# GpSimd instead of VectorE makes the sixteen sums of the base weights' quadrants

## Chip, cores and metric

One core of one Trainium2 chip runs the program. The metric is the device time of one execution in microseconds (us), as the median of the runs shown. Engines are named as in the profile: PE (TensorE matmul), PEld (its weight load), DVE (VectorE), ACT (ScalarE), POOL (GpSimd), SP (the queue that issues most DMAs).

## What is computed

```python
q_emb = relu(cond @ W3 + b3)                      # 16 x 1024
v_sum = sum(x, axis=1)                            # x: 16 x 512 x 1024
y = relu(((512 * x + v_sum) * q_emb[:, None]) @ W2 + b2)
base = y @ W_base + b_base
shared = (y @ A_s) @ B_s
gates = softmax(y @ W_router + b_router)          # 6 experts, the best two kept
routed = sum over e of ((y @ A_r[e]) * w_e) @ B_r[e]
out = x + base + shared + routed
```

Both 1024 x 1024 products, with W2 and with W_base, take nearly all the work. The other terms are of rank 16 to 112.

## The kernel before, in words

The 16 batches go in 8 pairs through a W2 stage (pair numbers g = 0 to 7, i = g in the code) and then again 8 pairs through a W_base stage (g = 8 to 15, p = g - 8). Activations lie transposed, features on partitions, 512 tokens in a row. A pair and a weight matrix, each cut in two by two quadrants, are multiplied in the Strassen-Winograd way: 7 products n = 0 to 6 in place of 8, each of 4 tiles in, 4 tiles out (`group(g, n, j)`, output tile j). Some pairs replace some of these products by another such step inside (`inner`). Every operand of a product is split in a high part rounded to fp32r (made by ACT, `high`, `wb_high`) and the rest (made by DVE, `low`, `wb_low`), and each tile product is three matmuls: high x high, low x high, high x low (`three`, lines 3062 to 3064). So a group is 12 matmuls.

The weights of W_base for the seven products are the quadrants themselves (n = 0, 1, 6) and four sums of quadrants, each made in four tiles k of 128x512. They are made while the last pair of the W2 stage (i = LAST = 7) and the first of the W_base stage (g = 8, p = 0) run:

- `wb_sum_1(k)`: Q21 + Q22, in place in `wl_raw[:, 2]`, the weights of product 3.
- `wb_sum_2(k)`: that less Q11, again in place, for product 2. It waits until `wb_low(3, k)` has read the first sum, and for Q11, which SP loads into `wh_raw[:, 2]` once all four `wb_sum_1` are counted (`sp.wait_ge(wb_sum, H)`, line 653).
- `wb_sum_4(k)`: Q12 less the tile of `wb_sum_2`, for product 4.
- `wb_sum_3(k)`: Q11 - Q21, for product 5.

One semaphore, `wb_sum`, counts all sixteen in this order, and `wb_high` on ACT waits for it (lines 1242 to 1259). `wl_raw` and `w_lo` have the same addresses, and so have `wh_raw` and `w_hi`: `wb_low(2, k)` overwrites the tile that `wb_sum_4(k)` reads. `wb_high(2, k)` stands in ACT's program between the `high(8, 0, j)` of the next pair and `y_high(7, C22, j)`, so what it waits for holds these up too.

The order of the work on each engine is written out by hand; engines meet at semaphores alone. On DVE, between the second and the last output tiles of pair 7, stand in turn `low(8, 0, j)`, `y_low(7, C22, j)`, `c21(7, j - 1)`, `t1(8, j)` and a sum. `y_low` (line 2048 for C22 and C21, line 2046 for C11 and C12) makes the low part of an output tile of the W2 stage, and PE's `project_y` (three matmuls, the router's and the experts' first factor) takes it directly behind one group: PE does group(7, 6, 0), project_y(7, C22, 0), group(7, 6, 1), project_y(7, C22, 1) and so on to project_y(7, C22, 3), and then group(8, 0, j), project_y(7, C21, j). The `c22` and `c21` steps (line 1991) add a PSUM bank to a tile in SBUF.

GpSimd makes a few small column vectors (`shift_of`, `shift2_of`) and issues DMAs of the inner steps' weights. In its program, between its last `shifts(7)` and the first `store_weights(7)`, stands nothing.

Of the kernel before, what the change touches and what calls it, by code (L numbers as in the profile page):

```python
# [7 lines left out]
ALU = mybir.AluOpType  # L8
# [19 lines left out]
H = 4  # L28
# [9 lines left out]
def adaln_ffn(nc, xT, condT, w3, w2, b2, wbase, bbase, acat, bcat, brouter, outT, E, R):  # L38
# [9 lines left out]
    LAST = NP - 1  # L48
# [10 lines left out]
    with ExitStack() as ctx:  # L59
# [47 lines left out]
        wh_raw = sb("wh_raw", [P, NPROD, H, T], F32, early)  # L107
        wl_raw = sb("wl_raw", [P, NPROD, H, T], F32, early)
# [768 lines left out]
        def _(pool):  # L877
# [128 lines left out]
            for e in range(EARLY):  # L1006
# [5 lines left out]
                if e + 1 < EARLY:  # L1012
                    load_partner(e + 1)
                    shift_of_partner(e + 1)
                    shifts(i + 2)

            for c in range(L2, 2 * L2):
                store_weights(c)
            for e in range(EARLY, len(QUADS)):
# [843 lines left out]
        def _(dve):  # L1863
# [339 lines left out]

            def wb_low(n, k):
                dve.wait_ge(wb_hi_done, wb_no(n, k))
                nc.vector.tensor_tensor(w_lo[:, n, k, :], wl_raw[:, 2 if n == 3 else n, k, :],
                                        w_hi[:, n, k, :].bitcast(F32), ALU.subtract).then_inc(wb_lo_done, 1)

# [12 lines left out]
            def inner_weight_sums(late):  # L2221
# [10 lines left out]
                nc.vector.tensor_tensor(iq11, iq22, iq11, ALU.subtract).then_inc(inner_w_sum, 1)  # L2232
                dve.wait_ge(inner_w_sum, sums_no(late, 3))
                nc.vector.tensor_tensor(iq12, iq12, iq11, ALU.subtract).then_inc(inner_w_sum, 1)

            def wb_sum_1(k):
                dve.wait_ge(wl_loaded[2], 16)
                dve.wait_ge(wh_loaded[2], 16)
                nc.vector.tensor_tensor(wl_raw[:, 2, k, :], wl_raw[:, 2, k, :], wh_raw[:, 2, k, :],
                                        ALU.add).then_inc(wb_sum, 1)  # L2240

            def wb_sum_2(k):

                dve.wait_ge(wb_lo_done, wb_lo_no(3, k))
                dve.wait_ge(wh_loaded[2], 32)
                nc.vector.tensor_tensor(wl_raw[:, 2, k, :], wl_raw[:, 2, k, :], wh_raw[:, 2, k, :],
                                        ALU.subtract).then_inc(wb_sum, 1)

            def wb_sum_4(k):
                dve.wait_ge(wb_sum, H + k + 1)  # L2250
                dve.wait_ge(wl_loaded[4], 16)
                nc.vector.tensor_tensor(wl_raw[:, 4, k, :], wl_raw[:, 4, k, :], wl_raw[:, 2, k, :],
                                        ALU.subtract).then_inc(wb_sum, 1)

            def wb_sum_3(k):
                dve.wait_ge(wl_loaded[5], 16)
                dve.wait_ge(wh_loaded[5], 16)
                nc.vector.tensor_tensor(wl_raw[:, 5, k, :], wl_raw[:, 5, k, :], wh_raw[:, 5, k, :],
                                        ALU.subtract).then_inc(wb_sum, 1)

            def inner_t1(r):
                e, n = RUNS[r]
# [292 lines left out]
            def pair(i):  # L2555
                if i == 0:
                    first_pair()
                else:
                    before_p4(i)
                    for j in range(H):  # L2560
                        low(i, 4, j)
                        if j == 1 and i not in QUADS:
                            gate_weights(i - 1, GA)
                        elif j == 2:
                            gate_apply(i - 1, GB)
                    if i in QUADS:
                        gate_logits(i - 1, GA)
                    y_low(i, C11, 0)
                    y_low(i, C11, 1)
                    if i == 1:  # L2570
                        inner_weight_low(0)
                        inner_weight_low(1)
                    if i == LAST:
                        for k in range(H):
                            wb_low(0, k)
                    for j in range(H):
                        low(i, 5, j)
                        if i in QUADS and j == 0:
                            gate_weights(i - 1, GA)
                        if j in (1, 2):  # L2580
                            y_low(i, C11, j + 1)
                        if i == LAST:
                            wb_sum_1(j)
                        if i == 1 and j == 0:
                            inner_weight_low(2)
                        elif i == 1 and j == 1:
                            inner_weight_sums(0)
                        elif i == 1 and j == 3:
                            inner_weight_low(3)
                    y_low(i, C12, 0)  # L2590
                    y_low(i, C12, 1)
                    for j in range(H):
                        low(i, 6, j)
                        if j == 0 and i == 1:
                            gate_apply(i - 1, GA)
                        if j > 0:
                            c22(i, j - 1)
                        if j >= 2:
                            y_low(i, C12, j)
                        if i == LAST:  # L2600
                            wb_low(3, j)
                        if i == 1 and j != 1:
                            inner_weight_low((4, 4, 5, 6)[j])
                    if i == LAST:
                        wb_low(1, 0)
                        wb_low(1, 1)
                    c22(i, H - 1)
                y_low(i, C22, 0)
                if joined(i):
                    gate_apply(i - 1, GA)  # L2610
                if i == LAST:
                    wb_sum_2(0)
                if i == 0:
                    c21(0, 0)
                    y_low(0, C22, 1)
                    low(1, 0, 0)
                    t1(1, 0)
                    low(1, 0, 1)
                    y_low(0, C22, 2)
                    c21(0, 1)  # L2620
                    low(1, 0, 2)
                    y_low(0, C22, 3)
                    low(1, 0, 3)
                    c21(0, 2)
                    for j in range(1, H):
                        t1(1, j)
                else:
                    for j in range(H):
                        low(i + 1, 0, j)
                        if j > 0 and i == LAST:  # L2630
                            y_low(i, C22, j)
                            c21(i, j - 1)
                        elif j > 0:
                            c21(i, j - 1)
                            y_low(i, C22, j)
                        t1(i + 1, j)
                        if i == LAST and j < H - 1:
                            wb_sum_2(j + 1)
                    if i == LAST:
                        wb_low(1, 2)  # L2640
                        wb_low(1, 3)
# [201 lines left out]
            def alone(p):  # L2843
                g = NP + p
                if p == 0:
                    y_low(LAST, C21, 0)
                for j in range(H):
                    low(g, 1, j)
                    if p == 0 and j > 0:
                        y_low(LAST, C21, j)  # L2850
                    t2(g, j)
                    if p == 0:
                        wb_sum_4(j)
                for j in range(H):
                    low(g, 2, j)
                    if p == 0 and j == 0:
                        gate_logits(LAST, GB)
                    if j == H - 1:
                        if p == 0:
                            dve.wait_ge(lr_hi_done, 1)  # L2860
                            nc.vector.tensor_tensor(low_lo[:], low_raw[:], low_hi[:].bitcast(F32),
                                                    ALU.subtract).then_inc(lr_lo_done, 1)
                            lr_low_a(p)
                    if j > 0:
                        c11(g, j - 1)
                    if p == 0:
                        wb_low(2, j)
                c11(g, H - 1)
                if p > 0:
                    lr_low_a(p)  # L2870
                for j in range(H):
                    low(g, 3, j)
                    t3(g, j)
                    t4(g, j)
                    if j > 0:
                        c11_add_low(p, j - 1)
                    if j == 0 and p == 0:
                        gate_weights(LAST, GB)
                    elif j == 2 and p == 0:
                        gate_logits(LAST, GA)  # L2880
                c11_add_low(p, H - 1)
# [99 lines left out]
            def pair2(p):  # L2981
# [26 lines left out]
                if g == SECOND - 1:  # L3008
                    inner_weight_sums(1)
                if p == 0:  # L3010
                    for k in range(H):
                        wb_sum_3(k)
                    for j in range(H):
                        low(g, 5, j)
                        wb_low(5, j)
# [451 lines left out]
```

## Time and profile before

| | |
|---|---|
| median of 3 runs | 1384.2 us (1383.12 to 1384.43) |
| profiled execution | 1387.79 us |
| its span, first to last instruction | 1386.0 us |
| PE busy | 1377.3 us, 99% of the span |
| DVE busy | 1089.7 us, 79% |
| ACT busy | 681.6 us, 49% |
| POOL busy | 87.0 us, 6% |
| granted clock of PE | 0.999 of full speed |

The profile is of one execution, whose instructions have a start and a duration each; all starts below are us from the start of the span. A DVE instruction of 128x512 is shown with 0.68 or 0.75 us, and back to back they start 0.60 or 0.66 us apart: the tail of one lies over the beginning of the next. The stretch in question is 650 to 760 us.

### The profile page before, as it was taken

To read this page: it belongs to the slowest core of one execution; us is meant where nothing else is said; L and a number is where in the kernel's file an instruction comes from. 1 tells how busy PE (TensorE), PEld (TensorE's weight loads), DVE (VectorE), ACT (ScalarE), POOL (GpSimd) and SP (SyncE) were. 2 spreads that over 40 slices of the span, in tenths; PEclk is the share of its full clock that TensorE was granted. 3 is DMA by queue.
4 is the path that set the end of the run, shared out by engine and by line. 5 is a ranking of instruction groups with operands and counts; after the bars stand their busy time and mean duration, and the time that the engine had idled before them with its cause. 6 is when DMAs were issued, how large, how long until landed. Compare 5 with 4: busy or idle time off the path is not lost.

```text
span 1386.0 us, 18469 instructions
## 1 busy us (share of the span) xinstructions
PE 1377.3 (99%) x6033; PEld 1129.4 (81%) x6033; DVE 1089.7 (79%) x1762; ACT 681.6 (49%) x1219; POOL 87.0 (6%) x184
## 2 busy tenths in 40 slices
PE   9999999999999999999999999999999999999998
PEld 6888888888888888888888888878788788888887
DVE  6977677675776757867889768988898878888797
ACT  7774765647556574665554233443334433344231
POOL 3000110000000000000000000110010100101000
PEclk9999999999999999999999999999999999999999
DMA  8253846545264451545836639879596694957845
GB/s 320 69 175 114 250 136 156 176 116 172 62 188 152 122 166 58 157 149 176 294 123 186 229 97 346 317 223 319 186 334 235 182 301 143 349 196 220 288 148 202
DMA packets 155888, 271.36 MB, mean 196 GB/s; under 512 B 40880, under 2 KB 41136, under 8 KB 155792
## 3 DMA queue, kind: packets, MB, share of 16 engines
q1 hardware_dynamic: 134048, 196.87, 43.6%
q0 software_dynamic: 16704, 60.82, 14.5%
q10 hardware_dynamic: 5040, 12.49, 2.4%
q8 instruction: 48, 0.79, 0.3%
q14 instruction: 48, 0.39, 0.1%
HBM read 183.75 MB, written 86.38 MB: 195 GB/s over the span
## 4 chain that ended last, share of the span: by engine, by line
PE 92%; DMA 3%; DVE 3%; issue 2%; ACT 0%; POOL 0%; SPq 0%; DVEq 0%; POOLq 0%; ACTq 0%
PE ps L3062 31%; PE ps L3064 31%; PE ps L3063 30%; DMA partner<-y_scratch 1%; DVE act_lo L1923 1%; DMA w_raw<-in_w 1%; DMA ha_raw<-hw_scratch 0%; DMA inner_scratch<-staged 0%; DVE act_lo L2347 0%; DVE buf L1991 0%; DVE buf L2392 0%; PE ps L3073 0%; DVE staged L2211 0%; DVE partner L2276 0%; DVE buf L2716 0%
## 5 line engine op out<-in xcount | busy, mean ns | idle before, releaser
L3062 PE MATMUL ps<-act_hi,w_hi 128*128 128x512 f32 x1408 | 549.0, 390 | 0.8 <-DVE act_lo L1923 0.7
L3064 PE MATMUL ps<-act_hi,w_lo 128*128 128x512 f32 x1408 | 548.5, 390 | 0.0
L3063 PE MATMUL ps<-act_lo,w_hi 128*128 128x512 f32 x1408 | 548.4, 389 | 0.0
L3062 PEld LDWEIGHTS ps<-act_hi,w_hi 128*128 128x128 f32 x1408 | 264.7, 188 | 58.0 <-DVE act_lo L1923 2.1
L3063 PEld LDWEIGHTS ps<-act_lo,w_hi 128*128 128x128 f32 x1408 | 264.8, 188 | 54.9
L3064 PEld LDWEIGHTS ps<-act_hi,w_lo 128*128 128x128 f32 x1408 | 264.6, 188 | 55.0
L1087 ACT ACTIVATE act_hi<-src 128x512 fp32r<-128x512 f32 x184 | 109.8, 622 | 85.4 <-PE ps L3064 81.4
L3062 PE MATMUL ps<-act_hi,inner_w 128*128 128x512 f32 x336 | 131.5, 391 | 0.2
L3063 PE MATMUL ps<-act_lo,inner_w 128*128 128x512 f32 x336 | 130.8, 389 | 0.0
L3064 PE MATMUL ps<-act_hi,inner_w 128*128 128x512 f32 x336 | 130.7, 389 | 0.0
L1923 DVE TENSOR_TENSOR act_lo<-src,act_hi 128x512 fp32r<-128x512 f32 x168 | 112.0, 686 | 14.5 <-ACT act_hi L1087 14.4
L1106 ACT ACTIVATE yhi<-buf 128x512 fp32r<-128x512 f32 x128 | 80.1, 626 | 79.5 <-PE ps L3064 78.9
L1991 DVE SCALAR_TENSOR_TENSOR buf<-ps,b_sb,buf 128x512 f32<-128x512 f32 x80 | 59.4, 748 | 42.0 <-PE ps L3064 42.0
L1916 DVE SCALAR_TENSOR_TENSOR act_lo<-src,shift,act_hi 128x512 fp32r<-128x512 f32 x104 | 76.6, 747 | 19.1 <-ACT act_hi L1084 19.1
L937 POOL DMA_DIRECT2D inner_w<-inner_scratch x84 | 45.1, 537 | 565.4 <-PE ps L3064 530.3
L3062 PEld LDWEIGHTS ps<-act_hi,inner_w 128*128 128x128 f32 x336 | 63.1, 188 | 16.0 <-DVE act_lo L2347 2.0
L1991 DVE SCALAR_TENSOR_TENSOR buf<-ps,bb_sb,buf 128x512 f32<-128x512 f32 x79 | 57.9, 746 | 23.0 <-PE ps L3064 21.1
L1084 ACT ACTIVATE act_hi<-src,shift 128x512 fp32r<-128x512 f32 x100 | 69.8, 714 | 11.4 <-PE ps L3064 9.4
L3064 PEld LDWEIGHTS ps<-act_hi,inner_w 128*128 128x128 f32 x336 | 63.1, 188 | 13.2
L3063 PEld LDWEIGHTS ps<-act_lo,inner_w 128*128 128x128 f32 x336 | 63.1, 188 | 12.9
L2046 DVE TENSOR_TENSOR buf_lo<-buf,yhi 128x512 fp32r<-128x512 f32 x64 | 43.5, 687 | 36.0 <-ACT yhi L1106 35.9
L1036 ACT ACTIVATE src<-src,qn 128x512 f32<-128x512 f32 x92 | 65.5, 712 | 4.8 <-DMA src<-in_xT 4.8
(189 smaller groups left out, 1752.8 us busy)
## 6 DMA issues: line engine op xcount, KB each, us to landing
src<-in_xT SPq DMA_DIRECT2D x224, 256.0 KB, 4.0
inner_w<-inner_scratch POOLq DMA_DIRECT2D x84, 512.0 KB, 4.3
y_scratch<-buf SPq DMA_DIRECT2D x128, 256.0 KB, 3.2
src<-y_scratch SPq DMA_DIRECT2D x128, 256.0 KB, 5.6
outT<-buf SPq DMA_DIRECT2D x91, 256.0 KB, 4.9
wl_raw<-in_wbase SPq DMA_DIRECT2D x8, 1024.0 KB, 6.4
inner_scratch<-staged POOLq DMA_DIRECT2D x14, 512.0 KB, 5.6
inner_scratch<-staged ACTq DMA_DIRECT2D x14, 512.0 KB, 6.0
```

The source lines that it names most:

```text
L937: pool.dma_start(inner_w[:, c % 2], inner_dram[kind, m]).then_inc(inner_w_loaded[c % 2], 16)
L1036: nc.scalar.activation(src[:, t, :], src[:, t, :], ACT.Identity, scale=qn[:, H * HALF_OF[q] + k, 2 * i + BATCH_OF[q]:2 * i + BATCH_OF[q] + 1],
L1084: nc.scalar.activation(act_hi[:, slot(g, n, k), :], source[:, t, :], ACT.Identity, bias=shift[:, t:t + 1]).then_inc(hi_done, 1)
L1087: nc.scalar.activation(act_hi[:, slot(g, n, k), :], source[:, t, :], func).then_inc(hi_done, 1)
L1106: nc.scalar.activation(yhi[:, (y_no(i, c, j) - 1) % 2, :], buf[:, j, :], func).then_inc(yhi_done, 1)
L1916: nc.vector.scalar_tensor_tensor(act_lo[:, s, :], source, shift[:, t:t + 1], act_hi[:, s, :].bitcast(F32), ALU.add, ALU.subtract).then_inc ...
L1923: nc.vector.tensor_tensor(act_lo[:, s, :], source, act_hi[:, s, :].bitcast(F32), ALU.subtract).then_inc(lo_done, 1)
L1991: nc.vector.scalar_tensor_tensor(buf, ps[:, bank, :], bias, buf, ALU.add, ALU.add).then_inc(done, 1)
L2046: nc.vector.tensor_tensor(lo, y, hi, ALU.subtract).then_inc(ylo_done, 1)
L3062: nc.tensor.matmul(out, wh, a_h, start=start, stop=False, skip_group_check=onto)
L3063: nc.tensor.matmul(out, wh, a_l, start=False, stop=False, skip_group_check=onto)
L3064: return nc.tensor.matmul(out, wl, a_h, start=False, stop=stop, skip_group_check=onto)
```

## The change

The sixteen sums leave DVE's program and stand in POOL's, in the same order, with the same waits, behind the last `shifts(7)`. `wb_low(2, k)` on DVE gets a wait on the count of `wb_sum_4(k)`, which the order of DVE's own program gave before. Nothing else is changed; ACT's and SP's waits on `wb_sum` are as they were.

```diff
@@ gpsimd
                     shift_of_partner(e + 1)
                     shifts(i + 2)
 
+            def wb_sum_1(k):
+                pool.wait_ge(wl_loaded[2], 16)
+                pool.wait_ge(wh_loaded[2], 16)
+                nc.gpsimd.tensor_tensor(wl_raw[:, 2, k, :], wl_raw[:, 2, k, :], wh_raw[:, 2, k, :],
+                                        ALU.add).then_inc(wb_sum, 1)
+
+            def wb_sum_2(k):
+                pool.wait_ge(wb_lo_done, wb_lo_no(3, k))
+                pool.wait_ge(wh_loaded[2], 32)
+                nc.gpsimd.tensor_tensor(wl_raw[:, 2, k, :], wl_raw[:, 2, k, :], wh_raw[:, 2, k, :],
+                                        ALU.subtract).then_inc(wb_sum, 1)
+
+            def wb_sum_4(k):
+                pool.wait_ge(wb_sum, H + k + 1)
+                pool.wait_ge(wl_loaded[4], 16)
+                nc.gpsimd.tensor_tensor(wl_raw[:, 4, k, :], wl_raw[:, 4, k, :], wl_raw[:, 2, k, :],
+                                        ALU.subtract).then_inc(wb_sum, 1)
+
+            def wb_sum_3(k):
+                pool.wait_ge(wl_loaded[5], 16)
+                pool.wait_ge(wh_loaded[5], 16)
+                nc.gpsimd.tensor_tensor(wl_raw[:, 5, k, :], wl_raw[:, 5, k, :], wh_raw[:, 5, k, :],
+                                        ALU.subtract).then_inc(wb_sum, 1)
+
+            for k in range(H):
+                wb_sum_1(k)
+            for k in range(H):
+                wb_sum_2(k)
+            for k in range(H):
+                wb_sum_4(k)
+            for k in range(H):
+                wb_sum_3(k)
             for c in range(L2, 2 * L2):
                 store_weights(c)
@@ vector
             def wb_low(n, k):
                 dve.wait_ge(wb_hi_done, wb_no(n, k))
+                if n == 2:
+                    dve.wait_ge(wb_sum, 2 * H + k + 1)
                 nc.vector.tensor_tensor(w_lo[:, n, k, :], wl_raw[:, 2 if n == 3 else n, k, :],
                                         w_hi[:, n, k, :].bitcast(F32), ALU.subtract).then_inc(wb_lo_done, 1)
@@ vector, pair(LAST)
-                        if i == LAST:
-                            wb_sum_1(j)
...
-                if i == LAST:
-                    wb_sum_2(0)
...
-                        if i == LAST and j < H - 1:
-                            wb_sum_2(j + 1)
@@ vector, the first pair of the W_base stage
                     t2(g, j)
-                    if p == 0:
-                        wb_sum_4(j)
...
                 if p == 0:
-                    for k in range(H):
-                        wb_sum_3(k)
                     for j in range(H):
                         low(g, 5, j)
```

The four functions that stood in VectorE's program are the same with `nc.vector` and `dve` in place of `nc.gpsimd` and `pool`.

## Rows read from the trace of the kernel before

**Rows 1.** The page, part 1: busy time of each engine.
```profile
PE 1377.3 (99%) x6033; PEld 1129.4 (81%) x6033; DVE 1089.7 (79%) x1762; ACT 681.6 (49%) x1219; POOL 87.0 (6%) x184
```
**Rows 2.** Waits, 640 to 790 us: who waited for whom, us in total, times, longest.
```profile
ACT w_hi L1258 <- DVE wl_raw L2246: 6.8, 3, 4.0
...
PEld ps L3062 <- DVE hb_lo L2658: 0.2, 1, 0.2
```
**Rows 3.** Instructions on `wl_raw`: ns min/median/max, first and last start (the four sums).
```profile
L2239 DVE TENSOR_TENSOR wl_raw<-wl_raw,wh_raw x4: 683/684/685, 662.7 to 668.2; 128x512 f32<-128x512 f32 x4
L2246 DVE TENSOR_TENSOR wl_raw<-wl_raw,wh_raw x4: 683/684/686, 686.6 to 694.6; 128x512 f32<-128x512 f32 x4
L2252 DVE TENSOR_TENSOR wl_raw<-wl_raw x4: 683/684/686, 701.3 to 708.5; 128x512 f32<-128x512 f32 x4
L2258 DVE TENSOR_TENSOR wl_raw<-wl_raw,wh_raw x4: 684/684/690, 751.4 to 753.2; 128x512 f32<-128x512 f32 x4
...
DMA to landing us min/median/max: 5.2/6.9/9.6
```
**Rows 4.** Instructions on `wh_raw`: its three loads, same columns, and their landing times.
```profile
L533 SPq DMA_DIRECT2D wh_raw<-in_wbase x3: 435/499/563, 651.7 to 687.6; - x3
...
DMA to landing us min/median/max: 5.6/8.7/10.2
```
**Rows 5.** Timeline of SP: the second of these loads (start, us taken to issue).
```profile
672.91 0.43 SPq L533 DMA_DIRECT2D wh_raw<-in_wbase x1
```
**Rows 6.** Timeline of POOL, first 3 us: start, duration.
```profile
0.72 0.20 POOL L879 MEMSET ident<- 128x128 f32 x1 [0.29 <-POOLq L3461]
...
0.92 0.52 POOL L881 MEMSET grow<- 128x512 f32 x1
...
2.07 0.28 POOL L885 TENSOR_SCALAR_AFFINE_SELECT ident<-ident 128x128 f32<-128x128 f32 x1
```
**Rows 7.** Timeline of POOL: small instructions beside a busy and beside an idle DVE.
```profile
26.87 0.50 POOL L906 TENSOR_TENSOR shift<-shift 128x1 f32<-128x1 f32 x1 [0.15 <-POOL shift L898]
...
99.05 0.74 POOL L906 TENSOR_TENSOR shift<-shift 128x4 f32<-128x4 f32 x1 [0.17 <-POOL shift L898]
...
354.82 0.20 POOL L906 TENSOR_TENSOR shift<-shift 128x4 f32<-128x4 f32 x1 [0.17 <-POOL shift L898]
```
**Rows 8.** Timeline of DVE: what ran beside the first two of these.
```profile
26.57 0.75 DVE L1916 SCALAR_TENSOR_TENSOR act_lo<-src,shift,act_hi 128x512 fp32r<-128x512 f32 x1
...
99.05 0.68 DVE L2048 SCALAR_TENSOR_TENSOR buf_lo<-buf,yhi 128x512 fp32r<-128x512 f32 x1
```
**Rows 9.** Timeline of DVE, 663 to 700 us: PSUM adds (L1991) and y_low.
```profile
663.88 0.68 DVE L2046 TENSOR_TENSOR buf_lo<-buf,yhi 128x512 fp32r<-128x512 f32 x1
...
681.35 0.75 DVE L1991 SCALAR_TENSOR_TENSOR buf<-ps,b_sb,buf 128x512 f32<-128x512 f32 x1 [0.85 <-PE ps L3064]
...
684.75 0.75 DVE L1991 SCALAR_TENSOR_TENSOR buf<-ps,b_sb,buf 128x512 f32<-128x512 f32 x1 [0.24 <-PE ps L3064]
685.41 0.68 DVE L2048 SCALAR_TENSOR_TENSOR buf_lo<-buf,yhi 128x512 fp32r<-128x512 f32 x1
...
689.63 0.68 DVE L2048 SCALAR_TENSOR_TENSOR buf_lo<-buf,yhi 128x512 fp32r<-128x512 f32 x1
...
692.69 0.68 DVE L2048 SCALAR_TENSOR_TENSOR buf_lo<-buf,yhi 128x512 fp32r<-128x512 f32 x1
...
695.76 0.69 DVE L2048 SCALAR_TENSOR_TENSOR buf_lo<-buf,yhi 128x512 fp32r<-128x512 f32 x1
...
699.49 0.68 DVE L2048 SCALAR_TENSOR_TENSOR buf_lo<-buf,yhi 128x512 fp32r<-128x512 f32 x1
```
**Rows 10.** Timeline of PE: first matmul of three of the project_y steps.
```profile
667.48 0.39 PE L3062 MATMUL ps<-yhi,a_hi 128*128 128x512 f32 x1
...
687.88 0.39 PE L3062 MATMUL ps<-yhi,a_hi 128*128 128x512 f32 x1
...
701.48 0.39 PE L3062 MATMUL ps<-yhi,a_hi 128*128 128x512 f32 x1
```

More of the change, by code:

```diff
@@ L2234, in inner_weight_sums @@
                 nc.vector.tensor_tensor(iq12, iq12, iq11, ALU.subtract).then_inc(inner_w_sum, 1)
[L2236 to L2259, printed above, removed]
             def inner_t1(r):
```

## The prediction

> **What bounds the kernel now.** I read the page first: PE is busy for 1377.3 of 1386.0 us [rows 1], so only an edit that makes PE wait, or ends a wait of PE, moves the time. Next I looked for such waits where the sums are made: in 640 to 790 us PE waits once for another engine, 0.2 us for the low part of `hb` [rows 2]. That part hangs on the gates and their DMAs, not on a sum, and moving sums from DVE brings nothing of it back. DVE's relief is real (16 x 0.60 us = 9.6 us, at 662.7 to 668.9, 686.6 to 695.3, 701.3 to 709.2 and 751.4 to 753.9 [rows 3]), but it is relief of an engine that PE does not wait for. So the change can gain at most about 0.2 us, and the question is what it can make late.
>
> **When POOL can run the sums.** In POOL's program the next step is `store_weights(7)`, whose data are made a pair later, so nothing is held up behind the sums. The first sum needs its loads into `wl_raw` and `wh_raw`; the later is issued at 651.7 and lands 10.2 us on, the longest of three [rows 4]: 661.9. `wb_sum_2` needs Q11: issued at 672.91 [rows 5], landed after 5.6 us [rows 4], so 678.5, some 8 us before DVE did this sum. `wb_sum_4` needs Q12, issued right behind that (some 0.8 us later) and landed within 9.6 us, the longest of its kind [rows 3]: by 683.3, and as its turn comes only at 686.6 (below) that does not bind. `wb_sum_3` needs a load issued at 687.6, landed at the median 8.7 us: 696.3 [rows 4]. POOL thus makes every sum no later than DVE did. What waits for a sum gains: ACT's 6.8 us for `wb_sum_2` [rows 2] go. SP's wait for four sums stays covered: its Q11 load is issued only at 672.91 [rows 5], behind a store, and POOL's first four end near 668. The new wait of `wb_low(2, k)` stands at 715 or later (behind the sums that end at 709.2 [rows 3]), against sums that POOL ends by 694: covered by some 20 us.
>
> **Price of one sum on POOL.** The trace before has none of this size. A memset of 128 columns takes 0.20 us, one of 512 takes 0.52 [rows 6]: 0.83 ns a column above 0.10 us. The select of 128 columns, which reads one operand and writes one, takes 0.28, so 1.4 ns a column [rows 6]. A sum reads one operand more: 0.10 + 512 x (1.4 + 0.7) ns = 1.2 us, of which I take 1.1 us as the time in which it reads. Low end: 0.52, a memset of the same size; high end: three streams at the memset's rate, 1.37 us. I take 1.1, as the select is the nearest row. The Trainium skill, GPSIMD Engine Reference, "3.1 Elementwise — side-by-side cycle accounting", states 4497 ns for 2048 columns; a quarter, 1.12 us, is an estimate by that page and would give the same sum.
>
> **Who blocks whom.** A POOL instruction on 4 columns takes 0.20 us beside an idle DVE, and 0.74 us where a DVE instruction with two SBUF inputs starts at the same moment, 99.05: it ends at 99.79, just behind DVE's 99.73 [rows 7, 8]. One of a single column, issued at 26.87 in the middle of a DVE instruction of 26.57 to 27.32, ends at 27.37 [rows 7, 8]. So POOL's reading waits for the end of DVE's instruction and then gets its turn. Columns this few can't show what DVE loses when POOL reads for 1.1 us. I take it that it works both ways: DVE waits for POOL's whole instruction, and where both have work they take turns. The low bound is that DVE loses nothing, the high bound that it loses 1.37 us for each sum. Instructions that read a PSUM bank and one SBUF tile (L1991) I take as free to run beside POOL. The Trainium skill, SBUF — State Buffer, "Who interferes with whom", says the same of both directions: the pair of ports is an exclusive lock, and a DVE instruction with two SBUF inputs contends with a POOL instruction that reads SBUF. The trace agrees for POOL waiting on DVE (0.74 against 0.20 us); for the other direction no row here shows it.
>
> **The sum.** PE takes y_low tiles on a fixed beat: project_y(7, C22, 0) starts at 687.88 and each next one 3.40 us on, to 701.48 [rows 10]; its second matmul, 0.23 us in, reads the low part. Without any change the margins are 2.0, 1.2, 1.5, 1.9 and 1.5 us (ends are starts + 0.68 [rows 9]). DVE's delay, against before:
>
> - First four sums, from 661.9. Three stand before y_low of C11, tile 2 (start 663.88 [rows 9]), with one of DVE's own gone: +3.3 - 0.6 = +2.7, end 667.3, needed at 667.48 + 0.23 = 667.7 [rows 10]. Just covered; a sum of over 1.25 us would break it.
> - To y_low(C22, 0), 685.41. POOL gets five turns (four `wb_sum_2`, one `wb_sum_4`): 5.5 us. Two lie beside L1991 and hide 0.66 each; DVE's idle before 681.35 and 684.75 (0.85 and 0.24, with the overlap of 0.08 each some 1.25) goes. 5.5 - 1.3 - 1.25 = +2.9. It ends at 689.0, needed at 688.1: **0.9 us late**.
> - To y_low(C22, 1), 689.63: three more `wb_sum_4`, +3.3, two of DVE's sums gone, -1.2: +5.0, end 695.3, needed at 691.5: **3.9 late**.
> - To y_low(C22, 2), 692.69: two `wb_sum_3`, +2.2, one DVE sum gone, -0.6: +6.6, end 699.95, needed at 694.9: **5.1 late**.
> - To y_low(C22, 3), 695.76: the last two, one half hidden by an L1991, +1.5, less 0.6: +7.5, end 703.95, needed at 698.3: **5.7 late**.
> - To y_low(C21, 0), 699.49: still +7.5, end 707.7, needed at 701.7: **6.0 late**.
>
> Each lateness is counted from the old beat, so they don't add up: PE ends 6.0 us behind. After that DVE wins back the four sums at 701 to 709 (-2.4) and then its idle time, and nothing is late again. The last four, at 751 to 754, go from DVE and cost nothing: ACT and DVE stand earlier there. Sum: +6.0 us; the profiled execution of 1387.8 would be 1393.8, and on the median of 1384.2, which lies 3.6 below it, 1390.2.
>
> At 0.52 us a sum nothing is late (0); at 0.85 the same steps give +3.0, at 1.37 +9.9 (y_low(C22, 1) then stands behind a `wb_sum_3` as well and is 7.4 late, y_low(C22, 2) 9.9).
>
> **Rivals.**
> A, not slower: POOL's reading does not hold DVE up, or for less than about 0.65 us a sum. Place: y_low(C22, 0) and (C22, 1). For it: no DVE instruction in [rows 8] is longer than its kind, though a POOL instruction ran into its end. Against it: POOL is plainly held by DVE. Price: 0, or -0.2 at best; 1384.2. With 0.65 to 0.84 us it would be +1 to +2.8. Together 0.38.
> B, slower by starving: POOL loses its turn again and again while DVE is dense. Then `wb_sum_2(0)` comes late, ACT's `wb_high(2, 0)` holds the y_high tiles behind it (it waited up to 4.0 us already [rows 2]), and each of the four tiles could cost a sum plus a split, 1.1 + 0.6: some 7 us, 1391. Against it: in [rows 7] POOL gets the very next turn. 0.06.
> C, dearer: a sum holds DVE for over 1.37 us; PE is late in the first window too, more than +10, over 1394. 0.05.
> D, faster by more than 0.2%: nothing in the trace offers it, since PE waits 0.2 us there. 0.02.
>
> **How the numbers follow.** A measurement can tell about 0.2%, 2.8 us, from no change. The forecast (lock both ways, 0.84 to 1.37 us) has 0.49: it is slower by over 0.2%. With B and C, slower is 0.60; A is same, 0.38; faster 0.02. As both signs hold much, the forecast's own range is 1387.0 to 1394.1; the full one reaches down to A's 1384 and leaves out C: 1383.6 to 1394.5.
>
> **What would show it.** Right: POOL's TENSOR_TENSORs start at about 662, 679, 686 and 696 and take over 1 us, longer where DVE had begun before; DVE instructions with two SBUF inputs are stretched to 1.2 to 1.9 us or start over 1 us apart at 662 to 703; PE waits for `buf_lo` (L2048) at 688 to 707, five times, 6 us together. If instead DVE's beat of 0.60 us holds and PE has no new wait, A is right. If ACT's wait for `wl_raw` grows, B. A wait of DVE at `wb_low(2, k)` would refute the cover that I gave it.

## The result and the profile after

The changed kernel takes 1390.5 us (median of 6 runs, 1389.27 to 1394.59) against 1384.3 before (6 runs, 1382.68 to 1386.38): ratio 1.0048, 95% interval 1.0033 to 1.0063. It is slower by 6.2 us, by more than the 2.8 us that a measurement can tell.

The page, part 1, of the changed kernel:

```profile
PE 1376.4 (99%) x6033; PEld 1128.0 (81%) x6033; DVE 1092.6 (79%) x1746; ACT 681.5 (49%) x1219; POOL 115.9 (8%) x200
```

Against [rows 1], DVE has 16 instructions less and is busy 2.9 us longer: the rows of those that are left have grown by more than the sums took. POOL has 16 more and 28.9 us, 1.8 us for each sum. The waits of 640 to 790 us, us in total, times, longest:

```profile
PEld ps L3061 <- DVE buf_lo L2080: 6.0, 3, 3.0
...
PE ps L3061 <- DVE buf_lo L2080: 4.7, 3, 2.6
...
PEld ps L3061 <- DVE buf_lo L2078: 0.2, 1, 0.2
```

PE had no wait for a `y_low` here before [rows 2]; now it has three for those of C22 and C21 (L2080 is the old L2048). ACT's wait for `wb_sum_2` [rows 2] is gone. PE's timeline, the same project_y steps as in [rows 10] and where PE waited; the first line is the step at 667.48 of before:

```profile
667.35 0.39 PE L3061 MATMUL ps<-yhi,a_hi 128*128 128x512 f32 x1
...
688.93 0.50 PE L3061 MATMUL ps<-yhi,a_hi 128*128 128x512 f32 x1 [0.91 <-DVE buf_lo L2080]
...
695.22 0.50 PE L3061 MATMUL ps<-yhi,a_hi 128*128 128x512 f32 x1 [2.58 <-DVE buf_lo L2080]
...
706.94 0.50 PE L3061 MATMUL ps<-yhi,a_hi 128*128 128x512 f32 x1 [1.24 <-DVE buf_lo L2080]
```

PE's beat is 0.13 us early at 667 and 5.46 us late at 706.94 against 701.48 [rows 10]. Taken from the starts of PE's matmuls, which before came 0.227 us apart without a gap in this stretch, the new gaps are 5.6 us in all: 1.1, 2.7 and 1.4 at these three places, and 0.1 at each of four matmuls near by. (Below, "new PE waits" is always this measure.) These gaps account for 5.6 of the 6.2 us; the rest lies within the interval. The two profiled executions alone differ by less, 1389.27 against 1387.79: that of before waited 2.2 us for `ha` at 986 us, with slower matmuls behind the wait, while this one waited 0.6 us at the same matmul with none slower. That wait has nothing to do with the sums.

What held DVE shows in its own timeline, in the stretch of the first two waits:

```profile
687.11 0.74 DVE L2023 SCALAR_TENSOR_TENSOR buf<-ps,b_sb,buf 128x512 f32<-128x512 f32 x1
687.77 1.11 DVE L2080 SCALAR_TENSOR_TENSOR buf_lo<-buf,yhi 128x512 fp32r<-128x512 f32 x1
688.80 1.77 DVE L2133 TENSOR_TENSOR h_a<-h_a,grow 128x512 f32<-128x512 f32 x1
690.50 1.78 DVE L1955 TENSOR_TENSOR act_lo<-src,act_hi 128x512 fp32r<-128x512 f32 x1
692.21 1.75 DVE L1971 TENSOR_TENSOR src<-src 128x512 f32<-128x512 f32 x1
...
694.48 0.68 DVE L2080 SCALAR_TENSOR_TENSOR buf_lo<-buf,yhi 128x512 fp32r<-128x512 f32 x1
```

and POOL's timeline (a row of several is their common span):

```profile
661.33 8.96 POOL L1020 TENSOR_TENSOR wl_raw<-wl_raw,wh_raw 128x512 f32<-128x512 f32 x4 [39.63 <-DMA wh_raw<-in_wbase]
678.64 5.09 POOL L1026 TENSOR_TENSOR wl_raw<-wl_raw,wh_raw 128x512 f32<-128x512 f32 x3 [8.35 <-DMA wh_raw<-in_wbase]
684.96 1.68 POOL L1026 TENSOR_TENSOR wl_raw<-wl_raw,wh_raw 128x512 f32<-128x512 f32 x1 [1.23 <-DVE w_lo L2240]
686.59 6.82 POOL L1032 TENSOR_TENSOR wl_raw<-wl_raw 128x512 f32<-128x512 f32 x4
699.29 7.05 POOL L1038 TENSOR_TENSOR wl_raw<-wl_raw,wh_raw 128x512 f32<-128x512 f32 x4 [5.88 <-DMA wh_raw<-in_wbase]
```

While POOL's four `wb_sum_4` (L1032) run, three DVE instructions with two SBUF inputs start 1.70 us apart in place of 0.60: each is held 1.10 us ("held": the start of the next comes that much later than without POOL). POOL's are shown with 1.7 us too, and start 1.70 apart: each engine's row holds its own 0.6 or 1.1 us and the other's turn. The PSUM add (a PSUM bank and one SBUF tile as inputs) at 687.11 (L2023, the old L1991) keeps its 0.74 us, and the y_low behind it is held only for what is left of POOL's turn (0.43 us). When POOL is done, at 693.4, DVE is at once back at 0.60.

### The profile page after: what moved, and what is told of

Read it like the earlier page. It is cut to its first block, busy times and chain, and to the rows that moved or that the text cites. A ratio compares the mean times of both kernels' runs of the same rounds, so it can differ in the third digit from the quotient of the medians.

```text
span 1387.3 us, 18473 instructions
## 1 busy us (share of the span) xinstructions
PE 1376.4 (99%) x6033; PEld 1128.0 (81%) x6033; DVE 1092.6 (79%) x1746; ACT 681.5 (49%) x1219; POOL 115.9 (8%) x200
## 4 chain that ended last, share of the span: by engine, by line
PE 90%; DVE 4%; issue 3%; DMA 2%; ACT 0%; SPq 0%; POOL 0%; DVEq 0%; POOLq 0%; ACTq 0%
PE ps L3061 30%; PE ps L3063 30%; PE ps L3062 30%; DMA partner<-y_scratch 1%; DMA inner_scratch<-staged 1%; DVE act_lo L1955 1%; PE ps L3072 1%; DVE buf L2023 0%; DMA ha_raw<-hw_scratch 0%; DVE w_lo L2240 0%; DVE act_lo L2356 0%; PE ps L3087 0%; DVE partner L2285 0%; DVE buf L2401 0%; DVE buf_lo L2080 0%
## 5 line engine op out<-in xcount | busy, mean ns | idle before, releaser
L1955 DVE TENSOR_TENSOR act_lo<-src,act_hi 128x512 fp32r<-128x512 f32 x168 | 114.9, 703 | 13.6 <-ACT act_hi L1119 13.5
L2023 DVE SCALAR_TENSOR_TENSOR buf<-ps,b_sb,buf 128x512 f32<-128x512 f32 x80 | 59.3, 747 | 42.1 <-PE ps L3063 42.0
L2023 DVE SCALAR_TENSOR_TENSOR buf<-ps,bb_sb,buf 128x512 f32<-128x512 f32 x79 | 57.8, 744 | 26.0 <-PE ps L3063 22.4
```

Source lines behind the costliest of these rows:

```text
L1955: nc.vector.tensor_tensor(act_lo[:, s, :], source, act_hi[:, s, :].bitcast(F32), ALU.subtract).then_inc(lo_done, 1)
L2023: nc.vector.scalar_tensor_tensor(buf, ps[:, bank, :], bias, buf, ALU.add, ALU.add).then_inc(done, 1)
```

## The experiments

The theory: POOL's reading and a DVE instruction with two SBUF inputs exclude each other; each sum holds DVE 1.1 us, and the time is lost where such turns make a step of DVE late for PE. The rivals: the sums cost through being handed between engines (semaphores, order, POOL's issue), or each sum on POOL costs a fixed share of the 6 us wherever it stands. Each time is compared with the kernel before, on the same chip; "VectorE" and "GpSimd" in the expectations are DVE and POOL.

**A memset in place of each sum.** The sums are left out.

```diff
-                nc.gpsimd.tensor_tensor(wl_raw[:, 2, k, :], wl_raw[:, 2, k, :], wh_raw[:, 2, k, :],
-                                        ALU.add).then_inc(wb_sum, 1)
+                nc.gpsimd.memset(wl_raw[:, 2, k, :], 1.0).then_inc(wb_sum, 1)
```

> GpSimd does a memset of the same 128x512 tile in place of each of the sixteen sums, behind the same waits and with the same semaphore (so the sums themselves are left out). Lock theory (GpSimd's reading of two operands keeps VectorE's two-input instructions out, 1.1 us each time): a memset reads nothing, VectorE keeps its spacing of 0.60 us, PE's new waits at 688.9, 695.2 and 706.9 us (1.1, 2.7 and 1.4 us) are gone, time 1384.3 within 1.5 us. Rival (the new place of the sums, their semaphores and GpSimd's issue are what costs, whatever the instruction reads): PE still waits about 5 us between 684 and 708 us, time near 1390.

Measured: ratio 1.0003 (0.9994 to 1.0012), no new PE wait. POOL's rows of `wl_raw`, ns min/median/max:

```profile
L1020 POOL MEMSET wl_raw<- x4: 527/528/529, 662.4 to 663.8; 128x512 f32 x4
```

Memsets start at 683.40, 683.87 and 684.34 us, and DVE's three `wb_low` beside them keep their 0.60 us from start to start:

```profile
682.66 1.89 DVE L2236 TENSOR_TENSOR w_lo<-wl_raw,w_hi 128x512 fp32r<-128x512 f32 x3
```

A POOL instruction that only writes neither waits nor holds, in the same places with the same semaphores. So the handing over from engine to engine is not what costs. The kernel also shows that DVE's relief of sixteen instructions is worth nothing.

**Eight more additions on POOL, with all sums on DVE.** POOL adds each tile of the loaded Q12 to itself, in place and twice over, so the weights of product 4 come out wrong. A variant with sixteen additions into an unused tile gave no time and no trace, so it says nothing either way.

```diff
+            def extra(k, again):
+                if again:
+                    pool.wait_ge(grow_set, 2 + k + 1)
+                else:
+                    pool.wait_ge(wl_loaded[4], 16)
+                nc.gpsimd.tensor_tensor(wl_raw[:, 4, k, :], wl_raw[:, 4, k, :], wl_raw[:, 4, k, :],
+                                        ALU.add).then_inc(grow_set, 1)
+
+            for again in (False, True):
+                for k in range(H):
+                    extra(k, again)
@@ wb_sum_4 on VectorE
                 dve.wait_ge(wl_loaded[4], 16)
+                dve.wait_ge(grow_set, 2 + 2 * H)
```

> The kernel before, all its sums on VectorE, and GpSimd besides adds each tile of the loaded quadrant Q12 to itself in place, twice over (eight additions of 128x512, so Q12 is four times too large), from the landing of Q12 at about 682 us. VectorE's wb_sum_4 waits for them, but stands at 701 us, long after. Lock theory: eight turns of 1.1 us in the dense stretch, and VectorE keeps its own sums: y_low of C22 tile 0 is 1.4 us late and tile 1 5.2 more, 6.7 us of new PE waits between 687 and 698 us, time 1389 to 1392. Rival (the cost comes from handing the sums themselves to another engine): their order and their engine are as before, so 0, time 1384.3 to 1385.

Measured: 1391.8 us, ratio 1.0045 (1.0032 to 1.0058), 6.3 us of new PE waits, of them 4.7 at the two y_low. PE's timeline:

```profile
690.66 0.50 PE L3074 MATMUL ps<-yhi,a_hi 128*128 128x512 f32 x1 [1.16 <-DVE buf_lo L2059]
...
697.40 0.50 PE L3074 MATMUL ps<-yhi,a_hi 128*128 128x512 f32 x1 [3.01 <-DVE buf_lo L2059]
```

So additions on POOL make the loss with no sum moved; the memsets showed that it is not their writing. The first wait came near what was worked out (1.3 for 1.4 us), the second was 3.2 for 5.2; the remaining 1.6 us is PE's clock, below. Both had been worked out with 1.1 us for each turn, and these turns were shorter. DVE beside them:

```profile
690.52 1.52 DVE L2112 TENSOR_TENSOR h_a<-h_a,grow 128x512 f32<-128x512 f32 x1
691.97 1.52 DVE L2257 TENSOR_TENSOR wl_raw<-wl_raw,wh_raw 128x512 f32<-128x512 f32 x1
693.42 1.52 DVE L1934 TENSOR_TENSOR act_lo<-src,act_hi 128x512 fp32r<-128x512 f32 x1
```

They start 1.45 us apart, a hold of 0.85 and not 1.10: that the first wait fitted was luck in part. A tile added to itself holds DVE less than the sum of two different tiles; why is open.

**Fewer columns: half, and three quarters.** The rest of each sum is left out. Half is:

```diff
-                nc.gpsimd.tensor_tensor(wl_raw[:, 2, k, :], wl_raw[:, 2, k, :], wh_raw[:, 2, k, :],
+                nc.gpsimd.tensor_tensor(wl_raw[:, 2, k, 0:256], wl_raw[:, 2, k, 0:256], wh_raw[:, 2, k, 0:256],
```

> The changed kernel with each sum over the first 256 of the 512 columns only (the other half is left out). Lock theory: GpSimd holds VectorE for 0.55 to 0.6 us at a time, which the margins of the y_low tiles (1.2 to 2 us) and VectorE's shed sums take up: PE's new waits between 684 and 708 us 0 to 0.3 us in all, time 1384.3 to 1385.5. Rival (a fixed cost for each GpSimd instruction and its semaphores): more than half of the 5.2 us of waits stays, 1387 to 1390.

> The changed kernel with each sum over 384 of the 512 columns (the last quarter is left out). Lock theory: VectorE is held 0.83 us at a time, between the 0.55 of half the columns (no new PE wait) and the 1.10 of all (5.6 us of them): worked out in turns, 1.8 us of new PE waits between 684 and 708 us (1.2 to 3), time 1386 to 1387. The waits do not grow in proportion to the columns (that would be 4.2 us): they begin where the margins of y_low end. Rival, the cost in proportion to the columns: 4 us, 1388.5.

Measured, half: ratio 1.0007 (0.9998 to 1.0016), no new PE wait. Three quarters: 1.0019 (1.0010 to 1.0029), 2.5 us of new waits, 1.9 of them at 693.27. DVE of the latter, in the stretch of the `wb_sum_4`:

```profile
687.65 1.50 DVE L2133 TENSOR_TENSOR h_a<-h_a,grow 128x512 f32<-128x512 f32 x1
689.07 1.51 DVE L1955 TENSOR_TENSOR act_lo<-src,act_hi 128x512 fp32r<-128x512 f32 x1
690.50 1.51 DVE L1971 TENSOR_TENSOR src<-src 128x512 f32<-128x512 f32 x1
```

They start 1.42 us apart, so the hold is 0.82 us; with half the columns they start 1.15 apart, a hold of 0.55. With 1.10 for all columns that is 2.15 ns a column each time. PE's new waits are 0, 2.5 and 5.6 us, not in proportion: they begin where the margins end, at a hold between 0.55 and 0.82 us (the prediction had 0.65).

**One operand to read instead of two.** The sums are left out; a copy stands in place of each, for `wb_sum_1`:

```diff
+                nc.gpsimd.tensor_copy(wl_raw[:, 2, k, :], wl_raw[:, 2, k, :]).then_inc(wb_sum, 1)
```

> GpSimd copies each 128x512 tile onto itself in place of each sum (the sums are left out). What holds VectorE is the reading, so with one operand to read instead of two the hold should be about half, 0.5 to 0.7 us, and PE's new waits 0 to 0.3 us, time 1384.3 to 1385.5. Rival (any GpSimd instruction that reads holds VectorE for a fixed time, or the copy is as long as the sum): holds of 1.1 us and 5 us of waits, 1390.

Measured: ratio 1.0002 (0.9993 to 1.0011), no new PE wait. DVE:

```profile
688.07 1.09 DVE L2129 TENSOR_TENSOR h_a<-h_a,grow 128x512 f32<-128x512 f32 x1
689.09 1.10 DVE L1951 TENSOR_TENSOR act_lo<-src,act_hi 128x512 fp32r<-128x512 f32 x1
```

These start 1.02 us apart, a hold of 0.42 us, less than the half that I expected (0.5 to 0.7).

**Which of the sums cost.** First `wb_sum_1` and `wb_sum_3` alone on POOL, the latter behind `wb_sum_4`; then `wb_sum_2` alone; then `wb_sum_4` alone. The lines added on POOL in the first; the others are alike, and the next sum on DVE waits for the count, so the order stays:

```diff
+            for k in range(H):
+                wb_sum_1(k)
+            pool.wait_ge(wb_sum, 3 * H)
+            for k in range(H):
+                wb_sum_3(k)
```

> Only wb_sum_1 and wb_sum_3 are moved to GpSimd (eight of sixteen), wb_sum_2 and wb_sum_4 stay on VectorE; wb_sum_3 waits for wb_sum_4 and so runs from about 709 us, where VectorE idles 4.5 us. Lock theory: the cost is in the dense stretch 679 to 703 us alone, where GpSimd now does nothing: PE's new waits 0 (0.5 us at most at 667.7 us), time 1384.3 to 1385. Rival (each sum on GpSimd costs its share): half of the change's 6 us, near 1387.3.

> Only the four wb_sum_2 on GpSimd. Lock theory: four turns at 679 to 687 us, of which VectorE's idle time and the steps from PSUM take up most: 0.5 us of new PE wait (0 to 1) at y_low of C22 tile 0, time 1384.5 to 1386. Rival (each sum costs its share, a quarter of 6 us): 1386.

> Only the four wb_sum_4 on GpSimd; they wait for the last wb_sum_2 of VectorE, so they run at about 695 to 702 us. Lock theory: four turns, none of VectorE's own sums gone by then: y_low of C21 tile 0 (margin 1.5 us) is 2.2 us late (1.5 to 3), at 704 us, time 1386.5. Rival (each sum costs its share): 1.5 us, spread over them or at the handing over to ScalarE, and not at y_low.

Measured: sums 1 and 3: ratio 0.9998 (0.9990 to 1.0007), new PE waits 0. Sum 2: 1.0005 (0.9996 to 1.0014), 0.8 us. Sum 4: 1.0018 (1.0010 to 1.0027), 1.9 us, nearly all in one wait of PE:

```profile
704.15 0.50 PE L3068 MATMUL ps<-yhi,a_hi 128*128 128x512 f32 x1 [1.64 <-DVE buf_lo L2057]
```

In new PE waits these three kernels cost 0, 0.8 and 1.9 us, together 2.7, and the change 5.6. A fixed share for each sum is refuted: eight sums cost nothing, and four cost 1.9 us in one place. What the groups add to each other can't be read from the difference of 2.7 and 5.6, since they don't stand where the change has them: `wb_sum_4` ran from 696.20 us in place of 686.59, and `wb_sum_3` from 709.64 in place of 699.29, while in the change its turns stand right before the wait at 706.94.

**All sixteen on POOL, eight of them later.**

```diff
+            pool.wait_ge(lo_done, op_no(NP, 1, H - 1))
             for k in range(H):
                 wb_sum_4(k)
+            pool.wait_ge(lo_done, op_no(NP, 3, H - 1))
             for k in range(H):
                 wb_sum_3(k)
```

> All sixteen sums on GpSimd as in the change, but its wb_sum_4 wait until VectorE has made the last low part of product 1 of the next pair (about 707 us, just ahead of 4.5 us in which VectorE idles), and its wb_sum_3 until the last low part of product 3 (about 735 us). Lock theory: the eight turns leave the dense stretch; new PE waits 0.5 us (0 to 1), time 1384.3 to 1385.5, with as many sums on GpSimd as in the change. Rival (the number of sums on GpSimd, or its semaphores, costs): 1390.

Measured: ratio 1.0018 (1.0009 to 1.0027). New PE waits 1.7 us: 0.84 near 688 (that of `wb_sum_2`) and 0.83 near 751 that I had not expected, the larger part of it for the low part of `hb`, on DVE behind the four late `wb_sum_3` of 735 to 742 us:

```profile
751.61 0.50 PE L3067 MATMUL ps<-hb_hi,low_hi 128*128 128x512 f32 x1 [0.30 <-DVE hb_lo L2667]
```

So the direction was right, the size not: against 0 to 1 us of waits it had 1.7, and its ratio stands for some 2.5 us.

**Twelve on POOL, twice.** `wb_sum_2` stays on DVE; `wb_sum_3` stands right behind `wb_sum_4`, and in the second kernel it waits for the low part of `hb` (the last line added below, which the first has not):

```diff
             pool.wait_ge(lo_done, op_no(NP, 1, H - 1))
             pool.wait_ge(wb_sum, 2 * H)
             for k in range(H):
                 wb_sum_4(k)
+            pool.wait_ge(lr_lo_done, 3)
             for k in range(H):
                 wb_sum_3(k)
```

> Twelve of the sixteen sums on GpSimd: wb_sum_1 at 662 us as in the change, wb_sum_4 from about 707 us and wb_sum_3 right behind, over the 4.5 us in which VectorE idles; wb_sum_2 stays on VectorE. Lock theory: no turn falls where a y_low or the low part of hb is near its time: PE's new waits 0 to 0.3 us, time 1384.5 to 1385.5, the same as before. Rival (each sum on GpSimd costs its share of 6 us): 1388.8.

> The twelve sums of the last kernel on GpSimd again, wb_sum_1 and wb_sum_4 where they were, but wb_sum_3 only once VectorE has made the low part of hb, at about 750 us, so that its four turns no longer stand in front of the c11 additions at 715 to 719 us whose PSUM banks PE needs (a wait of 2.4 us there). Lock theory: the wait at 721 us goes, since it came from where the turns fell, and nothing near 750 to 757 us is within 2 us of its time: new PE waits 0 to 0.4 us, 2.5 us less than the last kernel, the same time as before within 1 us (1384.5 to 1386). Rival (twelve sums on GpSimd cost 2.5 us wherever they stand): 1388.

Measured: the first 1.0020 (1.0011 to 1.0028), with 2.5 us of new waits: a miss. I had looked at the margins of low parts only, and PE's matmul at 721.14 waited for a PSUM bank that DVE's add frees:

```profile
721.14 0.50 PE L3071 MATMUL ps<-act_hi,w_hi 128*128 128x512 f32 x1 [2.23 <-DVE buf L2017]
```

Its DVE timeline shows why:

```profile
714.67 0.95 DVE L1949 TENSOR_TENSOR act_lo<-buf,act_hi 128x512 fp32r<-128x512 f32 x1 [4.49 <-ACT act_hi L1113]
715.54 1.29 DVE L2086 TENSOR_TENSOR logits<-logits,br_sb 128x24 f32<-128x24 f32 x1
716.87 0.20 DVE L2089 TENSOR_REDUCE lmax<-logits 128x4 f32<-128x24 f32 x1
717.11 0.99 DVE L2091 TENSOR_TENSOR logits<-logits,lmax 128x24 f32<-128x24 f32 x1
717.99 1.84 DVE L2234 TENSOR_TENSOR w_lo<-wl_raw,w_hi 128x512 fp32r<-128x512 f32 x1
```

An instruction of 24 columns with two SBUF inputs, 0.2 us by itself, takes 1.29 when it has to wait for a turn of POOL. The one at 716.87 has one input and keeps its 0.20 us within POOL's turn of 716.74 to 718.03. The second kernel, with the same twelve sums, has no new wait: ratio 0.9996 (0.9987 to 1.0005). With the same number of sums, place alone makes the difference. It is as fast as the kernel before, not faster; none of the kernels was.

## Why the prediction was right, point by point

- **PE is the bound, DVE's relief is worth nothing**: right; the memset kernel shows it (1.0003).
- **The loads and waits.** Right for the first three groups: POOL's sums came due at 661.3 (661.9 predicted), 678.6 (678.5) and 686.6 (686.6). Wrong for the last, the step "`wb_sum_3` needs a load issued at 687.6": I took the issue as unmoved. It went out at 691.4. SP's queue of the changed kernel:

```profile
690.60 0.32 SPq L566 DMA_DIRECT2D hw_scratch<-h_a  x1
690.97 0.43 SPq L533 DMA_DIRECT2D wl_raw<-in_wbase  x1
691.44 0.56 SPq L533 DMA_DIRECT2D wh_raw<-in_wbase  x1
```

  The loads stand in SP's program behind the store of `h_a`, which waits for the DVE instruction of 688.80, itself held. So `wb_sum_3` began at 699.3, not at 696.3. The lateness worked out for y_low(C22, 2) and (C22, 3), 5.1 and 5.7 us, did not come: no turn of POOL stood right before these two, and PE did not wait again until y_low(C21, 0). So PE waited three times, not five. The end of the sum held, as the turns of all four `wb_sum_3` still came before y_low(C21, 0) was done.
- **The price of a sum**: 1.1 us of hold taken, 1.10 measured. The way to it was luck in part: one read costs 0.82 ns a column (the copy's hold of 0.42 us), near the 0.83 of the memset, but two reads cost 2.15 and not 2 x 0.82. Only the tile added to itself (0.85 us) came to twice the copy. The whole instruction takes more than the hold; beside an idle DVE, in the kernel with sums 1 and 3:

```profile
L1026 POOL TENSOR_TENSOR wl_raw<-wl_raw,wh_raw x4: 1287/1288/1292, 709.6 to 713.4; 128x512 f32<-128x512 f32 x4
```

  These start 1.25 us apart. The estimate from the Trainium skill's 4497 ns (GPSIMD Engine Reference, "3.1 Elementwise — side-by-side cycle accounting"), 1.12 us for the whole instruction, is near the hold but below these 1.25 us, and the measurement decides.
- **Who blocks whom**: right in both directions, and right that a PSUM add runs beside POOL (0.74 us at 687.11). That POOL holds DVE was the assumption on which all hung, and no row of before could show it. The Trainium skill (SBUF — State Buffer, "Who interferes with whom") has it as an exclusive lock; the 1.70 us beat of both engines agrees.
- **The sum.** Lateness against the old beat: y_low(C22, 0) 0.9 predicted, 1.05 measured (688.93 against 687.88); (C22, 1) 3.9 and 3.95 (695.22 against 691.27, the same matmul before); (C21, 0) 6.0 and 5.5. End: +6.0 predicted, +6.2 measured in the medians, 5.6 in the new waits.
- **The first window**: "just covered" was right in that PE did not wait, but for another reason than mine: POOL did not get its turns there (below).
- **The rivals.** A (DVE not held) fell to the 1.70 us beat. B (POOL passed over) did occur, at 661 to 664 us and for one DVE instruction at 699.42, where it harmed nobody; it never came to the loss again and again, nor to the 7 us, that B supposed. C fell, the hold being 1.10.
- **The new wait of `wb_low(2, k)`**: it held nothing up; the first of them started at 720.50, 5.6 us behind before's as all else, with `wb_sum_4` done at 693.4.

## What to carry to other kernels

Moving an elementwise step with two inputs from VectorE to GpSimd doesn't take it off VectorE where that is dense: VectorE is held by each such step (1.10 us for 128x512 here), longer than the 0.60 us it saves. Where GpSimd's turns fall into VectorE's idle time, or VectorE works from PSUM, they cost nothing here; nor did the turns of 751 to 758 us in the second kernel of twelve, which held VectorE where nothing that it makes was near its time. So give each group of them a wait that puts it there, and look at everything that VectorE makes behind it, the small instructions and the additions that free a PSUM bank as well as the operands. And if the engine that bounds the kernel, here PE, didn't wait for VectorE before, there is nothing to gain, only margins to lose.

## What was not expected of the hardware

- **POOL is passed over, at times.** Its first sum was due at 661.33 and took 4.30 us:

```profile
661.33 4.30 POOL L1020 TENSOR_TENSOR wl_raw<-wl_raw,wh_raw 128x512 f32<-128x512 f32 x1 [39.63 <-DMA wh_raw<-in_wbase]
```

  In between DVE ran five instructions 0.60 us apart, the last from 663.80, and only when it idled did POOL get in. At 679.08, between two like instructions, it had its turn at once. The other kernels show that this was no accident of one execution. Of the eight kernels whose POOL starts reading at 661 to 664 us, in seven the first instruction was passed over three to five times and its row shows 2.9 to 4.3 us; in that with three quarters of the columns it was due at 662.52 and got its turn at the next boundary. Only an instruction for which POOL came from idle was passed over; once POOL had a turn, it and DVE took turns. What decides about the first is open; no experiment went for it.
- **A wait of PE can cost more than its length.** In the kernel with eight more additions, PE's matmuls behind the wait of 3.0 us came 0.43 us apart for seven of them in place of 0.23, and the windows of 690 to 698, 698 to 702 and 702 to 710 us (the third number from the right is the granted clock) show it:

```profile
690.00:698.00 8.00, 4.33 (x18) 3.25 (x19) 8.00 (x10) 3.34 (x6) 4.39 (x4) 1.00 0.68 229
698.00:702.00 4.00, 4.00 (x12) 3.14 (x11) 4.00 (x8) 1.67 (x3) 0.00 (x0) 0.57 0.70 270
702.00:710.00 8.00, 8.00 (x37) 6.61 (x36) 7.72 (x14) 3.99 (x7) 0.00 (x0) 1.00 0.27 99
```

  A granted clock of 0.57 over these 4 us is mostly the lower of the two levels, 1.2 GHz, and cost 1.6 us; before it fell PE had waited 1.2 and 3.0 us. The changed kernel's own wait of 2.6 us at 695 was not followed by it. The kernel before shows the same behind its wait for `ha` at 986 us: seven matmuls 0.43 us apart. So two waits of like length can have different prices.
